# A state-space scan and the block behind it: earlier first units, a reordered mixing block, and step sizes added on TensorE in the last sequence

## The chip, the cores and the metric

The kernel runs on one core of a Trainium2 chip, in one launch. The metric is device time in microseconds (us). Five engines work side by side, each through its own list in order: TensorE (PE in the profile, PEld for its weight loads), VectorE (DVE), ScalarE (ACT), GpSimd (POOL) and SyncE (SP, which here issues all DMAs). They meet only at semaphores.

## The reference, cut to what matters

`x` is (2, 1024, 256). The kernel computes `x1 = x + attn(moe(x))` and then `x1 + ffn(sample(x1))`. `attn` is two state-space scans (Mamba), one over the sequence and one over its reverse, whose outputs are mixed by a gate:

```
delta = softplus(dt @ dt_w + dt_b)                       # the step sizes
h_t = exp(delta_t * A) * h_(t-1) + (delta_t * u_t) * B_t # 16 states for each of 512 channels
y_t = sum over the states of h_t * C_t;  y = (y + uc * Dp) * silu(z);  y_f or y_b = y @ outproj
g = sigmoid([y_f, y_b] @ gate_w + gate_b);  attn = (g * y_f + (1 - g) * y_b) @ proj_w + proj_b
```

`sample` divides |x1| by its sum over the sequence, takes exp, divides again, sums up along the sequence, counts how many sums lie below a random value, and keeps the elements of x1 that are at least as large as the one at that place. `ffn` needs its result in two layouts (`xt_s`, `xm_s`), each cut in a high and a low float32r part.

## The kernel before, in words

Four phases follow each other: experts (until 229 us), scan (`mamba_phase`, 229 to 1090 us), mixing (`mix_phase`, 1090 to 1163 us), feed-forward (`ffn_phase`, to the end).

**Scan.** There are 4 sequences `k` (2 batches times 2 directions), each 1024 long, and 4 channel blocks `dc` of 128: 16 periods `w`. A period has 16 units `s`, each a 128x1024 tile (32 channels times 4 states); rows `r` of a period are its units. For a unit:
- ScalarE: the decay, exp(delta * A), into one of two PSUM slots `hs` (`decay`, L1055). It waits until the unit two before has left its slot.
- GpSimd: `dbu` = (delta * u) * B, from the replicated step sizes `rep` (`inputs`, L1125). It may be at most four units ahead of the scan.
- VectorE: the scan itself (L1199).
- The product with C, into `hc`: VectorE makes it (`weigh`, L1211), except in units 0, 4, 8, 12, which GpSimd weighs (L1131) after the dbu of three units later (`POOL_LAG`). ScalarE may reuse the `hs` slot of a GpSimd unit as soon as the scan is done, of the others after the product.
- TensorE: four units at a time are summed over the states (`add_states`, L952), after all four products, in the order half, unit, so that its four 32-column tiles follow each other.

Between the units ScalarE and GpSimd prepare the step size of the next period: TensorE's `t`, then Abs and Relu (L1021, L1022), Exp and Ln, then `step_add` (L710, the two parts of softplus added) and `step_du` (L716, times u) on GpSimd behind the dbu of units 6 and 7 (8 and 9 in each sequence's last period). SP stores the result and loads it back 32-fold (`dd_rows`, `rep`). TensorE does its other work at fixed places of the period (`pe_chores`): `skip` (L938) and `z` (L910) first, then, by group of units, projections of the neighbouring sequences: `o` (L920) in period 12, the first gates `g` (L931) in period 14. All results but `ysum` go through two PSUM banks in turn (`pb`); the next user of a bank waits until ScalarE has read the last one. ScalarE reads `z` at unit 4, `o` at units 7, 8, 10 and 11 of period 12, `g` at units 8 and 13 of period 14, with table loads round them. VectorE closes a period with `gate_out` (L1190) after the scan of unit 1 of the next.

For period 0 nothing is loaded back: TensorE replicates delta and delta*u (L903), 16 results, and ScalarE copies each to `rep` (L1036) ahead of the first four decays.

**Mixing.** `first` halves of the mix for batch 0 are already made in the scan. TensorE's list: project batch 0 (L1378), the output projection of sequence 3 (L1389, second half first), the gates of batch 1 (L1399, L1402), its projections (L1378), then 16 turns (L1418, four 128x128 transposes each): x1 and sampled x1 of batch 0, then of batch 1. VectorE's list: residuals of batch 0 (L1559), the whole sampling chain of batch 0 (L1578 to L1591), the mix (L1548, L1551), the same for batch 1, then the low parts of the last turns (L1625). ScalarE copies every turn out of PSUM; for the sampled x1 of batch 0 it copies twice, and GpSimd makes the low part from the second copy (L1529). GpSimd also makes yf - yb (L1518). x1's turns go through two tiles, whose stores (L1356) must land before they are filled again.

## Time and profile before

| what | value |
|---|---|
| median of 3 runs | 1525.18 us (1520.16 to 1525.98) |
| the profiled execution, its own time | 1525.6 us |
| its span, first to last instruction | 1523.8 us |
| busy share of the span | PE 79%, DVE 76%, POOL 60%, ACT 51% |
| mean granted TensorE clock | 0.878 of full speed |
| mean DMA rate | 110 GB/s |

Read it by stage: in the span's 40 slices of 38 us, DVE stands at 9 tenths from the eighth slice to the 28th, the scan, with POOL beside it; PE stands at 9 tenths in the first five and the last nine. The shares of the whole span therefore say little. All times below are us from the span's start. In a timeline the columns are start, duration, engine, line, operation, output<-inputs, count, and in brackets the idle time before it and who ended it.

### The profile page before, as it was taken

What the parts mean: (1) busy time and instruction counts of PE and PEld (TensorE: products, weight loads), DVE (VectorE), ACT (ScalarE), POOL (GpSimd) and SP (SyncE); (2) the same over time, 40 slices, a digit from 0 to 9 for tenths busy, and PEclk for the clock granted to TensorE, in tenths of its full rate; (3) what the DMA queues carried; (4) which work ended last, traced back from release to release, by engine and by line L of the source; (5) the groups of instructions that cost most, each with busy time, mean ns of one, the idle gap of its engine ahead of it and who ended that gap; (6) DMA issues with size and microseconds to landing.
All of it is one profiled execution on the core that took longest, in us unless ns stands there. A gap on an engine that the chain in (4) does not pass through costs nothing. (4 is left out here: it accounts for less than half of the span.)

```text
span 1523.8 us, 14635 instructions
## 1 busy us (share of the span) xinstructions
PE 1196.4 (79%) x4932; PEld 667.1 (44%) x4932; DVE 1150.8 (76%) x1020; ACT 776.8 (51%) x1036; POOL 908.4 (60%) x405
## 2 busy tenths in 40 slices
PE   5999977798739897549987375464577999999998
PEld 4788832233203232113332021121235778787887
DVE  4433355999999999999999999999676554544544
ACT  4434366567545676556675465464245533333440
POOL 4420016999999999999999999999533000000000
...
GB/s 195 42 124 111 28 48 172 152 110 104 107 262 125 117 145 148 104 193 193 91 104 100 234 117 217 114 117 49 57 14 180 0 139 0 139 0 102 22 38 72
DMA packets 41824, 167.20 MB, mean 110 GB/s; under 512 B 5521, under 2 KB 10129, under 8 KB 29346
## 3 DMA queue, kind: packets, MB, share of 16 engines
...
HBM read 134.43 MB, written 31.98 MB: 109 GB/s over the span
## 5 line engine op out<-in xcount | busy, mean ns | idle before, releaser
L1125 POOL TENSOR_TENSOR scan_dbu<-scan_rep,scan_bc 128x1024 f32<-128x1024 f32 x256 | 597.0, 2362 | 38.5 <-ACT scan_rep L1036 33.6
L1199 DVE TENSOR_TENSOR_SCAN scan_hs<-scan_hs,scan_dbu 128x1024 f32<-128x1024 f32 x192 | 439.1, 2287 | 17.3 <-ACT scan_hs L1055 17.1
L1055 ACT ACTIVATE scan_hs<-scan_rep,scan_neg_a 128x1024 f32<-128x1024 f32 x256 | 285.3, 1118 | 324.8 <-DVE scan_hc L1211 299.1
L952 PE MATMUL scan_ysum<-scan_hc,scan_sel 128*32 128x512 f32 x1024 | 176.8, 823 | 225.6 <-DVE scan_hc L1211 225.5
L1211 DVE TENSOR_TENSOR scan_hc<-scan_hs,scan_bc 128x1024 f32<-128x1024 f32 x192 | 234.9, 1223 | 6.1
L952 PEld LDWEIGHTS scan_ysum<-scan_hc,scan_sel 128*32 128x32 f32 x1024 | 36.6, 132 | 345.3 <-issue 345.3
L1131 POOL TENSOR_TENSOR scan_hc<-scan_hc,scan_bc 128x1024 f32<-128x1024 f32 x64 | 150.9, 2358 | 12.8 <-DVE scan_hc L1199 12.5
L1199 DVE TENSOR_TENSOR_SCAN scan_hc<-scan_hs,scan_dbu 128x1024 f32<-128x1024 f32 x64 | 145.8, 2278 | 9.0 <-ACT scan_hs L1055 8.7
L861 PE MATMUL scan_pb<-late_xin,scan_inwf 128*128 128x512 f32 x256 | 113.8, 598 | 0.0
L32 PE MATMUL ffn_sl<-ffn_tanh_s,xm_s 128*128 128x512 f32 x384 | 106.0, 411 | 2.3 <-DVE ffn_tanh_s L1926 2.3
L32 PE MATMUL moe_first<-moe_x_s,moe_w_s 128*128 128x512 f32 x384 | 97.7, 397 | 8.3 <-DVE moe_w_s L412 8.3
L418 DVE TENSOR_TENSOR moe_first<-scan_bc,moe_first 128x512 f32<-128x512 f32 x48 | 33.3, 695 | 92.5 <-ACT scan_bc L330 55.6
L1746 PE MATMUL ffn_oy<-ffn_y,ffn_et 128*128 128x256 f32 x448 | 101.3, 379 | 0.8 <-DVE ffn_y L1946 0.8
L32 PE MATMUL ffn_lg<-phi_s,xt_s 128*128 128x512 f32 x384 | 97.9, 404 | 2.5 <-PEq L1279 1.8
L1909 DVE TENSOR_REDUCE ffn_lmax<-ffn_lsb 128x2 f32<-128x1024 f32 x32 | 39.0, 1220 | 78.1 <-ACT ffn_lsb L1840 78.1
L1746 PEld LDWEIGHTS ffn_oy<-ffn_y,ffn_et 128*128 128x128 f32 x448 | 84.9, 190 | 13.5 <-DVE ffn_y L1946 1.3
L32 PEld LDWEIGHTS moe_first<-moe_x_s,moe_w_s 128*128 128x128 f32 x384 | 73.7, 193 | 25.1 <-issue 9.2
L32 PE MATMUL moe_second<-moe_hid_s,moe_w_s 128*128 128x512 f32 x288 | 75.4, 398 | 5.8 <-DVE moe_hid_s L423 5.6
L32 PEld LDWEIGHTS ffn_lg<-phi_s,xt_s 128*128 128x128 f32 x384 | 71.2, 191 | 18.4 <-issue 3.4
L861 PEld LDWEIGHTS scan_pb<-late_xin,scan_inwf 128*128 128x128 f32 x256 | 47.5, 190 | 67.5 <-issue 67.5
L32 PEld LDWEIGHTS ffn_sl<-ffn_tanh_s,xm_s 128*128 128x128 f32 x384 | 69.4, 188 | 15.7 <-DVE ffn_tanh_s L1926 3.0
L330 ACT ACTIVATE scan_bc<-moe_first 128x512 f32<-128x512 f32 x48 | 28.8, 599 | 89.2 <-PE moe_first L32 89.2
...
## 6 DMA issues: line engine op xcount, KB each, us to landing
...
```

What stands on the lines that cost most here:

```text
L32: mm = nc.tensor.matmul(out, lhs[x], rhs[y], start=first and i == 0, stop=last and i == 2)
L330: nc.scalar.activation(act_h[:, g % 2, :], first[:, g % 3, 0, :], ACT.Silu if g % UNITS < SU else ACT.Gelu).then_inc(act_done, 1)
L418: nc.vector.tensor_tensor(first[:, g % 3, 1, :], act_h[:, g % 2, :], first[:, g % 3, 1, :], ALU.mult).then_inc(hid_done, 1)
L861: mm = nc.tensor.matmul(out, inwf[:, q % IWR, c, t, :], xin[k % 2][:, c, h * CT + t:h * CT + t + CT], start=(t == 0 and c == 0), stop=(t = ...
L952: mm = nc.tensor.matmul(ysum[i * D32:(i + 1) * D32, h, :], sel[:], hc[:, (s0 + i) % HCR, h * CT:(h + 1) * CT], start=False, stop=last, til ...
L1055: nc.scalar.activation(hs[:, s % HSR, :], rep[:, e % REPS, 0, :], ACT.Exp, scale=neg_a[:, k % 2, NI * dc + i, r // NI:r // NI + 1]).then_i ...
L1125: nc.gpsimd.tensor_tensor(dbu[:, s % DBR, :], rep[:, e % REPS, 1, :], bc[:, j, 0, :], ALU.mult).then_inc(dbu_done, 1)
L1131: nc.gpsimd.tensor_tensor(hc[:, s % HCR, :], hc[:, s % HCR, :], bc[:, s % UPP // NI, 1, :], ALU.mult).then_inc(pool_hc_done, 1)
L1199: nc.vector.tensor_tensor_scan(states, hs[:, s % HSR, :], dbu[:, s % DBR, :], 0.0, ALU.mult, ALU.add).then_inc(scan_done, 1)
L1211: nc.vector.tensor_tensor(hc[:, s % HCR, :], hs[:, s % HSR, :], bc[:, r // NI, 1, :], ALU.mult).then_inc(hc_done, 1)
L1746: mm = nc.tensor.matmul(bank[:, b * DM:(b + 1) * DM], et[:, b, j, m * P:(m + 1) * P], y[:, j, b, :], start=(j == 0), stop=(j == JT - 1))
L1909: nc.vector.tensor_reduce(lmax[:, m, :], lsb[:, m % 2], AX_X, ALU.max, negate=True).then_inc(small, 1)
```

## The change

Three things, none of which changes what is computed (sums of float32 are formed in another order).

**First units.** In period 0 ScalarE makes the first four decays straight from the replicated delta in PSUM, two Exp of 512 columns each, instead of copying it; only delta*u is copied. VectorE makes the dbu of units 0 and 1 itself. For units 4 and on of that period delta comes back through DRAM: SP stores it and loads it (without delta*u) before the later rows of B and C.

**Last sequence.** In periods 12, 13, 14 TensorE adds the two parts of the next step size (two float32 products with the identity for each half, key `a`), after the sum of units 0 to 3; ScalarE copies the result to `dd` at unit 6; GpSimd's `step_du` comes after the dbu of unit 9, and it has no `step_add` there. GpSimd weighs units 0, 3, 7, 10, 13. In period 15 TensorE makes three of four parts of sequence 3's output projection for the second half before the last group (`op`, in the two `pb` banks, which stay reserved over the phase), and the last group is added unit by unit.

**Mixing.** The output projection only adds the missing part for the second half. yf - yb moves to VectorE, between the steps of batch 0's sampling, and the mix and the sampling are interleaved. The normalising pass (L1579) is left out: the running sum is of the unnormalised values and the reciprocal is multiplied in the comparison, against the random value less 0.001. The turns of sampled x1 of batch 0 come first, then those of its low part `xt_s[1]` (TensorE turns it, ScalarE copies it: 20 turns instead of 16, each copied once), then x1 of both batches, then sampled x1 of batch 1. x1's turns have four tiles. The first piece of `phi` is loaded and cut first, and the Exp table is loaded right after the last Sigmoid.

```diff
+POOL_UNITS, LATE_POOL_UNITS = (0, 3, 7, 10, 13), (0, 4, 8, 12)
...
+def late_step(w):
+    return w < DC * (GROUPS - 1) or w % DC == DC - 1
...
+    return r in (LATE_POOL_UNITS if late_step(s // UPP) else POOL_UNITS)
...
+    total = [("a", k, p + 1, h) for h in range(HALVES)] if r == 1 and not late_step(DC * k + p) else []
...
+    partial = [("op", k, cc, 0) for cc in range(KC)] if not more and (p, r) == (DC - 1, NJ - 1) else []
+    return partial + total + (old.get((p, r), []) if done else []) + (new.get((p, r), []) if more else []) + step + gates
...
+TOTAL_AT = 6
+POOL_STEP_AT, LATE_POOL_STEP_AT, TOTAL_POOL_STEP_AT = (6, 7), (8, 9), (None, 9)
...
+        self.banks = ctx.enter_context(nc.psum_tensor("late_banks", [P, 2, CT], F32))
...
+        pb = late.banks
...
+        def wait_delta(eng, w):
+            if w == 0 or late_step(w - 1):
+                eng.wait_ge(delta_done, own_adds(w))
+            else:
+                freed(eng, *(("a", *divmod(w, DC), h) for h in range(HALVES)))
...
+                kinds = slice(0, 1 if w == 0 else 2)
+                wait_delta(sp, w)
+                if w > 0:
+                    sp.wait_ge(du_done, w + 1)
+                sp.dma_start(dd_rows[w % 2][:, kinds], dd[:, kinds]).then_inc(dd_out, 16)
...
+                kinds = 1 if w == 0 else 2
+                sp.wait_ge(dd_out, 16 * (w + 1))
...
+                src = dd_rows[w % 2][i * D32:(i + 1) * D32, 0:kinds].rearrange("d k t -> d (k t)")
+                sp.dma_start(rep[:, e % REPS, 0:kinds].rearrange("p k t -> p (k t)"),
+                             src.unsqueeze(1).to_broadcast([D32, NG, kinds * SEQ])).then_inc(rep_in[e % REPS], 16)
...
-            for j in range(1, NJ):
+            store_step(0)
+            load_rows(0, 1)
+            for i in range(NI):
+                load_rep(0, i)
+            for j in range(2, NJ):
                 load_rows(0, j)
...
+            def step_total(k, dc, h):
+                out, done = claim(("a", k, dc, h))
+                pe.wait_ge(soft, (HALVES + 2) * (DC * k + dc + 1))
+                freed(pe, *(("t", k, dc, i) for i in range(HALVES)))
+                for i in range(2):
+                    mm = nc.tensor.matmul(out, ident[:], dd[:, i, h * CT:(h + 1) * CT], start=(i == 0), stop=(i == 1))
+                mm.then_inc(done, 1)
...
+            def out_partial(k, cc, _):
+                out, _ = claim(("op", k, cc, 0))
+                pe.wait_ge(yg_done, DC * (k + 1) - 1)
+                pe.wait_ge(outw_in, 16 * (k + 1))
+                for dc in range(DC - 1):
+                    nc.tensor.matmul(out, outw[:, dc, cc * P:(cc + 1) * P], uc[:, k % 2, dc, CT:2 * CT], start=(dc == 0), stop=False)
...
-                        pe.wait_ge(hc_done, by_dve(s + 1))
+                if s0 + NI < UNITS_ALL:
+                    for i in range(NI):
+                        wait_product(s0 + i)
                 last = s0 % UPP == UPP - NI
+                if s0 + NI == UNITS_ALL:
+                    for i in range(NI):
+                        s = s0 + i
+                        wait_product(s)
+                        for h in range(HALVES):
+                            mm = nc.tensor.matmul(ysum[i * D32:(i + 1) * D32, h, :], sel[:],
+                                                  hc[:, s % HCR, h * CT:(h + 1) * CT],
+                                                  start=False, stop=last, tile_position=(0, i * D32))
+                        mm.then_inc(ysum_done, 1)
+                    return
...
-                wait(act, dd_out, 16 * (w - 1))
+                wait(act, dd_out, 16 * w)
...
-                for kind in (1, 0):
-                    for h in range(HALVES):
-                        x, free = ready(act, "r", i, kind, h)
-                        nc.scalar.activation(rep[:, i, kind, h * CT:(h + 1) * CT], x, ACT.Copy).then_inc(free, 1)
+                for h in range(HALVES):
+                    x, free = ready(act, "r", i, 1, h)
+                    nc.scalar.activation(rep[:, i, 1, h * CT:(h + 1) * CT], x, ACT.Copy).then_inc(free, 1)
+            def step_total(k, dc, h):
+                x, free = ready(act, "a", k, dc, h)
+                nc.scalar.activation(dd[:, 0, h * CT:(h + 1) * CT], x, ACT.Copy).then_inc(free, 1)
...
-                    wait_rep(act, e)
+                if NI <= s < 2 * NI or w > 0 and r < NI:
+                    act.wait_ge(rep_in[e % REPS], 16 * (e // REPS + 1))
...
-                nc.scalar.activation(hs[:, s % HSR, :], rep[:, e % REPS, 0, :], ACT.Exp,
-                                     scale=neg_a[:, k % 2, NI * dc + i, r // NI:r // NI + 1]).then_inc(da_done, 1)
+                scale = neg_a[:, k % 2, NI * dc + i, r // NI:r // NI + 1]
+                if s < NI:
+                    for h in range(HALVES):
+                        x, free = ready(act, "r", i, 0, h)
+                        nc.scalar.activation(hs[:, s % HSR, h * CT:(h + 1) * CT], x, ACT.Exp, scale=scale).then_inc(free, 1)
+                else:
+                    nc.scalar.activation(hs[:, s % HSR, :], rep[:, e % REPS, 0, :], ACT.Exp, scale=scale).then_inc(da_done, 1)
...
+                    if r == TOTAL_AT and not late_step(w):
+                        for h in range(HALVES):
+                            step_total(k, p + 1, h)
...
-                    inputs(s)
+                    if s >= DVE_INPUTS:
+                        inputs(s)
...
+            def inputs(s):
+                wait_du(dve, s)
+                dve.wait_ge(bc_in[0], 2 * 16)
+                nc.vector.tensor_tensor(dbu[:, s % DBR, :], rep[:, s, 1, :], bc[:, 0, 0, :], ALU.mult).then_inc(dbu_done, 1)
...
+                    if UPP * w + r < DVE_INPUTS:
+                        inputs(r)
                     scan(UPP * w + r)
...
-        dif = uc[:, 1, 0:KC, :]
-        whole = uc[:, 1, KC:2 * KC, :].rearrange("p k (h t) -> p (k h) t", h=CB)
-        turn_sb = first.inwz
-        pg = ps("pg", [P, CB, KC, CT])
+        dif = late.y_first
+        turn_sb = [tile[:, q, :] for tile in (first.inwz, first.dtw_wide) for q in range(2)]
+        pg = ps("pg", [P, KC, CT])
...
+        TURNS = [(kind, b, j) for kind, b in (("high", 0), ("low", 0), ("x1", 0), ("x1", 1), ("high", 1)) for j in range(TG)]
+        X1_TURNS = [g for g, key in enumerate(TURNS) if key[0] == "x1"]
...
+            sp.dma_start(kept["phi"][:], a["phi"][:, :, 0:CT]).then_inc(kept["loaded_phi"], 16)
             sp.dma_start(iota[:], a["iota"].partition_broadcast(P)).then_inc(consts_in, 16)
             sp.dma_start(x1_late[:], a["xT"][:, :, SEQ:2 * SEQ]).then_inc(loaded_x, 16)
             sp.dma_start(kept["ident"][:], a["ident"]).then_inc(consts_in, 16)
-            sp.dma_start(kept["phi"][:], a["phi"][:, :, 0:CT]).then_inc(kept["loaded_phi"], 16)
...
+                    g = X1_TURNS[TG * b + j]
+                    sp.wait_ge(turn_read[g % 2], g // 2 + 1)
+                    sp.dma_start(x1_rows[:, b, 2 * j:2 * j + 2, :], turn_sb[j].rearrange("p (m d) -> p m d", m=2)
...
+                    for dc in range(DC - 1 if h else 0, DC):
+                        mm = nc.tensor.matmul(late_bank(cc) if h else pp[:, cc, :], outw[:, dc, cc * P:(cc + 1) * P],
+                                              uc[:, 1, dc, h * CT:(h + 1) * CT], start=(dc == 0), stop=(dc == DC - 1))
...
-            def turn(g):
-                b, kind, j = g // (2 * TG), g // TG % 2, g % TG
-                if kind == 0:
+            def turn(kind, b, j):
+                g = TURNS.index((kind, b, j))
+                if kind == "x1":
                     pe.wait_ge(res_done, KC * CB * (b + 1))
+                elif kind == "high":
+                    pe.wait_ge(xm_done, KC * (b + 1))
                 else:
-                    pe.wait_ge(xm_done, KC * (b + 1))
+                    pe.wait_ge(xt_low, KC * (b + 1))
                 if g >= 2:
                     pe.wait_ge(turn_read[g % 2], g // 2)
                 for q in range(4):
                     cc, m = q % 2, 2 * j + q // 2
-                    src = x1[b][:, cc, :] if kind == 0 else xm_t[b][:, cc, :]
-                    mm = nc.tensor.transpose(tr[:, g % 2, q * P:(q + 1) * P], src[:, m * P:(m + 1) * P], kept["ident"][:])
+                    rows = slice(m * P, (m + 1) * P)
+                    src = {"x1": x1[b][:, cc, rows], "high": xm_t[b][:, cc, rows], "low": xt_s[1][:, cc, b, rows].bitcast(F32)}[kind]
+                    mm = nc.tensor.transpose(tr[:, g % 2, q * P:(q + 1) * P], src, kept["ident"][:])
                 mm.then_inc(turned, 1)
...
-                    if b or j >= 2:
-                        act.wait_ge(x1_stored[j % 2], 16 * (b * TG // 2 + j // 2))
-                    nc.scalar.activation(turn_sb[:, j % 2, :], tr[:, g % 2, :], ACT.Copy).then_inc(turn_read[g % 2], 1)
+                if kind == "x1":
+                    if b:
+                        act.wait_ge(x1_stored[j % 2], 16 * TG // 2)
+                    nc.scalar.activation(turn_sb[j], tr[:, g % 2, :], ACT.Copy).then_inc(turn_read[g % 2], 1)
...
+                    copied = nc.scalar.activation(xm_s[kind == "low"][:, b, 2 * j:2 * j + 2, :],
+                                                  tr[:, g % 2, :].rearrange("p (m d) -> p m d", m=2), ACT.Copy)
+                    copied.then_inc(turn_high if b else turn_read[g % 2], 1)
...
+            act.wait_ge(kept["loaded_phi"], 16)
+            nc.scalar.activation(kept["phi_s"][0][:], kept["phi"][:], ACT.Copy).then_inc(phi_high, 1)
...
             sigmoids(0)
+            sigmoids(1)
+            nc.scalar.preload_act_table_set("exp_and_others")
             for u in range(KC):
                 piece_high(u)
-            sigmoids(1)
...
+            for key in TURNS[:-TG]:
+                turned_out(*key)
...
+            for key in TURNS[-TG:]:
+                if key[2] == 2:
...
-            pool.wait_ge(late.yf_in, 16)
-            pool.wait_ge(out_read, KC * CB)
-            for h in range(CB):
-                for k in range(KC):
-                    nc.gpsimd.tensor_tensor(own(k, h), forward(k, h), reverse(k, h), ALU.subtract).then_inc(dif_done, 1)
...
-            for j in range(TG):
-                g = TG + j
-                pool.wait_ge(turn_read[g % 2], g // 2 + 1)
-                tile = (slice(None), 0, slice(2 * j, 2 * j + 2), slice(None))
-                nc.gpsimd.tensor_tensor(xm_s[1][tile], whole[:, j, :].rearrange("p (m d) -> p m d", m=2),
-                                        xm_s[0][tile].bitcast(F32), ALU.subtract).then_inc(low_done, 1)
             piece_low(nc.gpsimd, pool, KC)
...
+            def difference(h):
+                dve.wait_ge(late.yf_in, 16)
+                dve.wait_ge(out_read, KC * (h + 1))
+                for k in range(KC):
+                    nc.vector.tensor_tensor(own(k, h), forward(k, h), reverse(k, h), ALU.subtract).then_inc(dif_done, 1)
...
+            def sums(b):
                 for cc in range(KC):
                     dve.wait_ge(exp2_done, KC * b + cc + 1)
-                each(lambda cc, s: nc.vector.reciprocal(s[:, 4:5], s[:, 3:4]))
...
-                each(lambda cc, s: nc.vector.tensor_tensor_scan(cum[:, cc, :], ones[:], share[:, cc, :], 0.0,
...
-                                                           ALU.mult, ALU.add))
+                each(b, lambda cc, s: nc.vector.reciprocal(s[:, 1:2], s[:, 3:4]))
+                each(b, lambda cc, s: nc.vector.tensor_tensor_scan(cum[:, cc, :], ones[:], share[:, cc, :], 0.0,
+                                                                   ALU.mult, ALU.add))
...
+                each(b, lambda cc, s: nc.vector.scalar_tensor_tensor(share[:, cc, :], cum[:, cc, :], s[:, 1:2],
+                                                                     rv[:, cc, b:b + 1].to_broadcast([P, SEQ]), ALU.mult, ALU.is_le,
+                                                                     accum_out=s[:, 4:5]))
...
+            link(nc.vector.tensor_scalar(rv[:], rv[:], 0.001, None, ALU.subtract))
...
+            sums(0)
+            difference(0)
             threshold(0)
+            difference(1)
+            mix(0)
+            choose(0)
+            mix(1)
             half_sum(0)
-            mix(0)
-            mix(1)
...
+            sums(1)
             threshold(1)
+            choose(1)
             half_sum(1)
```

## Rows read from the trace of the kernel before

**Rows 1.** Busy time of each engine while sequence 3 is scanned

```profile
core 0: us, PE busy (x) PEld busy (x) DVE busy (x) ACT busy (x) POOL busy (x), PEclk, DMA share, GB/s
877.00:1088.00 211.00, 114.41 (x392) 35.49 (x392) 204.01 (x116) 105.65 (x109) 206.24 (x91) 0.73 0.29 111
```

**Rows 2.** Timeline of DVE, start of period 12; the ends of periods 11 and 14

```profile
876.74 2.28 DVE L1199 TENSOR_TENSOR_SCAN scan_hc<-scan_hs,scan_dbu 128x1024 f32<-128x1024 f32 x1
878.93 2.27 DVE L1199 TENSOR_TENSOR_SCAN scan_hs<-scan_hs,scan_dbu 128x1024 f32<-128x1024 f32 x1
881.12 1.21 DVE L1190 TENSOR_TENSOR late_uc<-scan_ysum,scan_sz 128x1024 f32<-128x1024 f32 x1
...
886.83 2.29 DVE L1199 TENSOR_TENSOR_SCAN scan_hs<-scan_hs,scan_dbu 128x1024 f32<-128x1024 f32 x1
...
890.29 2.28 DVE L1199 TENSOR_TENSOR_SCAN scan_hc<-scan_hs,scan_dbu 128x1024 f32<-128x1024 f32 x1
...
1037.60 1.21 DVE L1190 TENSOR_TENSOR late_uc<-scan_ysum,scan_sz 128x1024 f32<-128x1024 f32 x1
```

**Rows 3.** Timeline of POOL, period 12: `step_add` after the dbu of unit 6

```profile
888.53 2.35 POOL L710 TENSOR_TENSOR scan_dd<-scan_dd 128x1024 f32<-128x1024 f32 x1
890.85 2.36 POOL L1125 TENSOR_TENSOR scan_dbu<-scan_rep,scan_bc 128x1024 f32<-128x1024 f32 x1
```

**Rows 4.** Timelines of PE, DVE, POOL and ACT at the start of the scan

```profile
241.39 3.80 PE L903 MATMUL scan_pb<-scan_dd,scan_hc 128*128 128x512 f32 x8 [0.60 <-ACT scan_rep L1036]
...
240.85 2.29 DVE L1199 TENSOR_TENSOR_SCAN scan_hc<-scan_hs,scan_dbu 128x1024 f32<-128x1024 f32 x1 [8.73 <-ACT scan_hs L1055]
...
262.53 2.30 DVE L1199 TENSOR_TENSOR_SCAN scan_hs<-scan_hs,scan_dbu 128x1024 f32<-128x1024 f32 x1 [2.41 <-ACT scan_hs L1055]
...
250.75 2.35 POOL L1125 TENSOR_TENSOR scan_dbu<-scan_rep,scan_bc 128x1024 f32<-128x1024 f32 x1 [2.03 <-ACT scan_rep L1036]
...
252.87 1.12 ACT L1055 ACTIVATE scan_hs<-scan_rep,scan_neg_a 128x1024 f32<-128x1024 f32 x1
```

**Rows 5.** Timeline of PE, periods 13 and 14: group sums and first gates

```profile
942.25 1.92 PE L952 MATMUL scan_ysum<-scan_hc,scan_sel 128*32 128x512 f32 x16 [0.75 <-DVE scan_hc L1211]
...
1010.22 7.13 PE L931 MATMUL scan_pb<-late_uc,scan_inwf 128*128 128x512 f32 x16
1020.24 3.49 PE L952 MATMUL scan_ysum<-scan_hc,scan_sel 128*32 128x512 f32 x16 [2.88 <-DVE scan_hc L1211]
```

**Rows 6.** Timeline of PE, the last group of the scan

```profile
1085.18 3.44 PE L952 MATMUL scan_ysum<-scan_hc,scan_sel 128*32 128x512 f32 x16 [8.93 <-DVE scan_hc L1211]
```

**Rows 7.** Mixing: timelines of PE and ACT, then three groups of DVE passes

```profile
1097.41 7.03 PE L1389 MATMUL mix_pg<-late_uc,late_outw 128*128 128x512 f32 x16
...
1129.90 3.70 PE L1378 MATMUL mix_tr<-late_uc,scan_inwf 128*128 128x512 f32 x8 [1.43 <-DVE late_uc L1551]
...
1135.59 1.28 ACT L1462 ACT_TABLE_LOAD   x1
...
1142.94 1.22 ACT L1472 ACTIVATE scan_inwz<-mix_tr 128x512 f32<-128x512 f32 x2 [2.71 <-DMA x_rows<-scan_inwz]
...
1156.90 1.97 PE L1418 MATMUL mix_tr<-ident,late_uc 128*128 128x128 f32 x8 [5.33 <-DVE late_uc L1591]
...
1163.22 2.04 PE L32 MATMUL ffn_lg<-phi_s,xt_s 128*128 128x512 f32 x4 [1.76 <-PEq L1279]
...
L1585 DVE SCALAR_TENSOR_TENSOR scan_bc<-mix_iota,mix_stat,scan_bc 128x1024 f32<-128x1024 f32 x4 | 6.9, 1752 | 0.1
L1582 DVE SCALAR_TENSOR_TENSOR scan_bc<-scan_bc,late_rv 128x1024 f32<-128x1024 f32 x4 | 5.8, 1487 | 0.1
L1579 DVE TENSOR_SCALAR scan_bc<-scan_bc,mix_stat 128x1024 f32<-128x1024 f32 x4 | 2.8, 750 | 0.1
```

**Rows 8.** Busy time while TensorE has nothing but turns

```profile
1144.00:1147.00 3.00, 2.59 (x12) 1.95 (x11) 2.97 (x4) 2.22 (x5) 1.03 (x1) 0.50 0.48 178
1149.00:1152.00 3.00, 2.42 (x15) 1.50 (x13) 2.96 (x5) 1.42 (x3) 3.00 (x2) 0.88 0.35 127
```

122 lines of the change are left out of this document (51 added, 71 removed).

## The prediction

> **What bounds the kernel now.** The slices of the page come first: PE full in the first and the last stage, DVE and POOL full in the scan between. So the next view is the busy time of the stage that the change touches most, sequence 3's scan [rows 1]: in 211 us DVE is busy for 204 and POOL for 206, both nearly full, ACT half, and TensorE's granted clock averages 0.73, a mixture of its two levels, 2.4 GHz (1.00) and 1.2 GHz (0.50). The timeline of DVE [rows 2] shows what a unit costs. A unit whose product GpSimd makes takes 2.19 us (876.74 to 878.93), one whose product DVE makes 3.46 (886.83 to 890.29), `gate_out` 1.1. Periods 12 to 14 take 156.5 us from `gate_out` to `gate_out` (881.12 to 1037.60), 52.2 each. On POOL a step has a pitch of 2.32 us (888.53 to 890.85) [rows 3]; 16 dbu, 4 products, `step_add` and `step_du` make 22 steps, 51.0 us: POOL is 1.2 us from being the bound. The start of the scan and the mixing block are chains over several engines, where the waits in brackets tell what came last [rows 4, 7]. The feed-forward phase starts at 1163.22 and is not touched; what is gained ahead of it moves it as a whole.
>
> **First units.** Now TensorE makes four replicated results in 3.80 us, 0.95 each, then stands 0.60 because ScalarE, in the decay (1.12), does not free a bank [rows 4]: 4.4 us per unit. After, ScalarE's decay is two half Exp on the results themselves (0.6 to 0.7 each, as its copies), so the chain is TensorE's 3.8 us per unit. The first scan gains the 1.1 us of the decay, the fourth decay, now 252.87 to 253.99, ends after three shorter rounds near 251.1. Behind it stand Abs and Relu of period 1, decay 4, and z, which TensorE starts later than ScalarE's table load ends: they move up by 1.8 us only, since z's own products need 1.7 us for each half. So unit 5's scan, which now waits 2.41 us for ScalarE until 262.53, comes at 260.8. POOL, without a gap from 250.75 on, now starts that unit 3 dbu when its replica is copied, near 249.25: 1.5 us earlier, and it feeds units 10 to 13 with little to spare. DVE's own two dbu (1.22 each, as its product) lie in its idle time. SP's store and four loads of delta start at 230.9, land some 6 us each behind one another, and are needed near 253: at nothing, with some 7 us of cover; the rows of B and C behind them are needed from 254 on. **Term: -1.5 us** (-0.5 to -2.5).
>
> **Last sequence.** Saved on DVE: one product in each of three periods, 3.46 - 2.19 = 1.27, in all -3.8. POOL's steps stay 22: the add leaves, the product comes, so its 51.0 us per period is a floor, but it starts each period several units ahead and can give that up for a while: the dbu of unit 6 is done at 888.5 [rows 3], 8 us before its scan. The price is a new chain. Times now from the scan of unit 0:
> - Unit 3 is GpSimd's. Its scan ends at 12.4 (10.1 to 12.4), its product by GpSimd at 15.0. Before, DVE's own product let TensorE's first sum begin at 13.8 (942.25 in period 13, whose unit 0 is one period after 876.74), after 0.75 us of idling, at the high clock, 1.92 us; after 2.88 us of idling such a sum took 3.49, the low clock [rows 5]. z ends 0.75 us before 13.8, so TensorE now idles 2 to 3 us. I take the low clock in periods 12 and 14 and half of it in 13: the sum ends at 18.6 (17.7).
> - `a`: four float32 products of 512 columns. Eight such took 7.13 us right after a slow sum [rows 5], 0.89 each: 3.55 us, the second half ready at 22.3, copied (0.6) at 22.9, then decay 7 (1.12) at 24.0. Unit 7's scan is due at 23.0 (two units of 2.19, five of 3.46, `gate_out`). Stall 1.0 us in 12 and 14, 0.2 in 13. With all at the high clock none, with `a` also at the low one 3.5 more in each.
> - Behind the waiting ScalarE stand `o` and `g`, which need the banks that `a` holds. Period 12: `o` takes four products from 22.1, ready at 25.8, copied, decay 8 at 27.5, due at 26.2: 1.3. Period 14: two gates, ready at 29.3, a Sigmoid 0.7, table load 1.28, decay 9 at 32.4, due at 29.7; such a stall is 0.5 now: 2.2 more.
> - `step_du` moves from behind dbu 7 to behind dbu 9, with store and loads behind it on SP. The last period of each sequence has it there already; the next period's first dbu is 15 us later. At nothing.
>
> Sum 1.0 + 1.3 + 0.2 + 1.0 + 2.2 - 3.8 = 1.9. **Term: +2.0** (-1.7 with every step at the high clock, +12 with `a` at the low one).
>
> **End of the scan.** Now the last sum begins after 8.93 us of idling, at the low clock: 3.44 us on the path [rows 6]. After, `op` (six products, 5.3 us) runs from about 1076, in DVE's shadow, and keeps TensorE busy; then units 12 to 14 are added as they come. Unit by unit four passes of one column tile follow each other (16 in 1.92 us is four at a time, 0.43 to 0.48 a pass), so unit 15 still takes 1.8 us at the high clock. **Term: -1.4** (+2 if `op` is slow and the sums queue behind it).
>
> **Mixing** [rows 7]. TensorE's list, up to the end of the last projection (1133.6), has one gap, 1.43 us. Six of the eight products of 7.03 us leave: -5.2. VectorE's mix is now done before its projection is due, so the gap goes: -1.4; sum -6.6. VectorE's moved differences (4 x 0.65) lie where it waited for gates. From there the chain is ScalarE and VectorE: the table load of 1.28 is made earlier; the two passes of L1579 in batch 1 (1.4) are gone; and the eight passes of L1582 and L1585, 12.9 us, would take 10.0 at the 1.22 to 1.28 of such a pass without GpSimd's L1529 beside it, which is gone too: -2.9. The sampled x1 of batch 1 is ready 6.6 + 1.3 + 1.4 + 2.9 = 12.2 earlier, at 1144.7 instead of 1156.9. But ScalarE is free only from 1131.3 (1135.59, the load, two Exp of 1.2, less 6.6 and 1.3) and must by then have copied 16 turns. A turn of four transposes takes TensorE 0.97 us at the low clock (8 in 1.97) and 0.6 to 0.7 at the high one with the bank's return; with five slow and nine fast ones behind the two that wait ready, the chain ends at 1143.5, and x1's second batch must wait for a store (ScalarE now waits up to 2.71 us for one): 1145. Then a copy of 1.05 and the tail, as now 5 us from the first high turn to the feed-forward. So it starts near 1151.7. **Term: -11.3** (-8 to -13). Twenty turns instead of 16 lie in this chain.
>
> One rule speaks against it. While TensorE had only turns, its clock was 0.50 for 3 us at 86% busy, and then 0.88 [rows 8]: here they do raise it, late. The Trainium skill's TensorE: Matmul & The Clock Gate, Part 4 (PE-mode transpose), says that transposes do not count as busy work for the clock. By it all turns would stay slow and the total be 1.3 us more, 1514.7; the second row disagrees.
>
> **Sum.** 1525.6 (the profiled execution's own time; the median of the runs is 1525.18, 0.4 lower) - 1.5 + 2.0 - 1.4 - 11.3 = 1513.4.
>
> **Rivals.**
> - *Clean*: TensorE stays fast, `a` is in time. Last sequence -1.7: 1509.7. For: sums after 0.75 us of idling are fast. Against: 2.88 us was enough to slow one.
> - *Slow a*: it runs at the low clock in part, +7 instead of +2: 1518.4; the product of unit 3 is then the step to blame.
> - *Turns*: ScalarE's 20 copies and the stores become the mixing block's bound, its gain is 7: 1517.7. Against: the longest such wait is 2.71 us, with two tiles instead of four.
> - *Cold* (the other side): all added work of sequence 3 at 1.2 GHz. It decides if TensorE, busy half of the time there, never gets back to 1.00. `a` +12; `op` takes 10.3 us, until 1086.6, and four sums of 2.6 to 3.4 follow, 1098 instead of 1088.6: +9. Total 1525.6 - 1.5 + 12 + 9 - 11.3 = 1533.8. Against: eight products right after a slow sum ran fast [rows 5].
> - *Nothing at the front*: POOL's queue or SP's loads hold back period 0, 1514.9: inside the forecast's range.
>
> **How the numbers follow.** Forecast 0.58 (its own range 1509 to 1518), clean 0.15, slow 0.14, turns 0.08, cold 0.05. The range 1507.5 to 1521.5 holds all but cold and the edges. 0.5% of 1525.18 is 7.6 us, about what a measurement of this kernel can tell from no change: faster means below 1517.6. That is nearly all of the forecast and of clean, under half of slow and of turns: 0.76; slower is cold, 0.04; the rest 0.20.
>
> **What would show it.** Feed-forward starts near 1151; between the second projection and it no GpSimd pass L1529; xm of batch 1 ready 2 us or less before ScalarE reaches it. In periods 12 to 14 DVE waits for the decay of units 7, 8 and 9, with `a`'s copies just before; without such waits the periods take 51 us and the stall term was wrong. The first scan comes near 239.7, unit 5's near 260.8; if that one has not moved, z or the loads bound it. A last sum of 3.4 us after the last product says that `op` did not keep the clock up. I am wrong if the mixing block gives less than 8 us or sequence 3 costs over 8.

## The result, and the profile after

The kernel after takes 1511.18 us (median of 5 runs, 1510.42 to 1512.48), the kernel before 1525.18 beside it (1520.07 to 1526.24): a ratio of 0.9918, 95% interval 0.9897 to 0.9939. The profiled execution takes 1510.97 us with a span of 1509.2, against 1525.6 and 1523.8. The prediction was 1513.4 in 1507.5 to 1521.5.

The two spans, cut at the same instructions. `du` is `step_du` of period 0 on VectorE, the last step before the scan's first units.

| stage | before | after | difference | predicted |
|---|---|---|---|---|
| start to `du` | 230.90 | 233.23 | +2.3 | 0 |
| `du` to `gate_out` of period 11 | 650.22 | 647.39 | -2.8 | -1.5 |
| periods 12 to 14 | 156.48 | 155.00 | -1.5 | +2.0 |
| period 15 | 51.17 | 49.43 | -1.7 | -1.4 |
| `gate_out` of period 15 to the mixing block | 1.70 | 1.69 | 0 | 0 |
| mixing block to the feed-forward's first product | 72.75 | 61.61 | -11.1 | -11.3 |
| feed-forward | 360.58 | 360.85 | +0.3 | 0 |

Start of the scan in the kernel after, timelines of PE, then DVE (the counterparts of rows 4; columns: start, length, engine, line, operation, tiles, shape, count, idle before it with its releaser):

```profile
234.60 16.37 PE L941 MATMUL late_banks<-scan_dd,scan_hc 128*128 128x512 f32 x32 [5.97 <-DVE scan_dd L740]
...
238.81 1.22 DVE L1278 TENSOR_TENSOR scan_dbu<-scan_rep,scan_bc 128x1024 f32<-128x1024 f32 x1 [4.35 <-ACT scan_rep L1102]
240.69 2.29 DVE L1286 TENSOR_TENSOR_SCAN scan_hc<-scan_hs,scan_dbu 128x1024 f32<-128x1024 f32 x1 [0.65 <-ACT scan_hs L1129]
...
261.45 2.30 DVE L1286 TENSOR_TENSOR_SCAN scan_hs<-scan_hs,scan_dbu 128x1024 f32<-128x1024 f32 x1 [2.14 <-ACT scan_hs L1131]
```

TensorE makes all 32 matmuls of the replicas without a gap. Unit 5's scan comes 28.2 us after `du` (31.6 before) and still waits for ScalarE, whose decay stands behind the reading of z.

Period 12 and the wait of period 14 in the kernel after, timelines of PE, ACT, DVE (rows 2, 3 and 5):

```profile
891.43 1.92 PE L1019 MATMUL scan_ysum<-scan_hc,scan_sel 128*32 128x512 f32 x16 [2.43 <-POOL scan_hc L1211]
893.28 3.70 PE L949 MATMUL late_banks<-scan_dd,scan_ident 128*128 128x512 f32 x8
...
897.02 0.60 ACT L1106 ACTIVATE scan_dd<-late_banks 128x512 f32<-128x512 f32 x1 [1.12 <-PE late_banks L949]
897.52 1.11 ACT L1131 ACTIVATE scan_hs<-scan_rep,scan_neg_a 128x1024 f32<-128x1024 f32 x1
...
899.37 2.28 DVE L1286 TENSOR_TENSOR_SCAN scan_hc<-scan_hs,scan_dbu 128x1024 f32<-128x1024 f32 x1
902.16 2.30 DVE L1286 TENSOR_TENSOR_SCAN scan_hs<-scan_hs,scan_dbu 128x1024 f32<-128x1024 f32 x1 [0.51 <-ACT scan_hs L1131]
...
931.86 1.21 DVE L1271 TENSOR_TENSOR late_uc<-scan_ysum,scan_sz 128x1024 f32<-128x1024 f32 x1
...
1008.91 2.30 DVE L1286 TENSOR_TENSOR_SCAN scan_hs<-scan_hs,scan_dbu 128x1024 f32<-128x1024 f32 x1 [1.79 <-ACT scan_hs L1131]
```

The first sum begins after 2.43 us of idling and still takes 1.92 us; it idles 2.18 us before that of period 13 and 2.28 before that of 14, and both take 1.92. `a` follows at once, is copied by 897.6, and the decay of unit 7 ends 0.7 us before its scan (899.37) begins: no wait.

End of the scan in the kernel after, PE and DVE (rows 6):

```profile
1074.10 5.42 PE L985 MATMUL late_banks<-late_uc,late_outw 128*128 128x512 f32 x12
1079.45 2.09 PE L1012 MATMUL scan_ysum<-scan_hc,scan_sel 128*32 128x512 f32 x12
1083.11 1.90 PE L1012 MATMUL scan_ysum<-scan_hc,scan_sel 128*32 128x512 f32 x4 [1.56 <-DVE scan_hc L1298]
...
1085.05 1.22 DVE L1271 TENSOR_TENSOR late_uc<-scan_ysum,scan_sz 128x1024 f32<-128x1024 f32 x1 [2.00 <-PE scan_ysum L1012]
```

Mixing in the kernel after, PE, ACT, DVE, then two groups of DVE passes (rows 7). No pass of GpSimd lies beside VectorE's threshold passes any more, and the L1677 and L1680 groups take 1.28 us a pass where rows 7 have 1.49 and 1.75:

```profile
1119.44 3.60 PE L1477 MATMUL mix_tr<-late_uc,scan_inwf 128*128 128x512 f32 x8
...
1139.05 1.21 ACT L1572 ACTIVATE scan_inwz<-mix_tr 128x512 f32<-128x512 f32 x2 [2.93 <-DMA x_rows<-scan_dtw]
...
1140.00 0.27 DVE L1695 TENSOR_SCALAR half_sum<-mix_stat 128x1 f32<-128x1 f32 x2
...
1148.35 2.04 PE L32 MATMUL ffn_lg<-phi_s,xt_s 128*128 128x512 f32 x4 [1.74 <-PEq L1368]
...
L1680 DVE SCALAR_TENSOR_TENSOR scan_bc<-mix_iota,mix_stat,scan_bc 128x1024 f32<-128x1024 f32 x4 | 5.0, 1282 | 0.1
L1677 DVE SCALAR_TENSOR_TENSOR scan_bc<-scan_bc,mix_stat,late_rv 128x1024 f32<-128x1024 f32 x4 | 5.0, 1280 | 0.0
```

The `half_sum` row marks the time at which the sampled x1 of batch 1 (xm) is ready: 53.3 us after the block's start at 1086.74. Below, stages are read in each run's own trace as in the table; most repeat to 0.1 us from run to run, while whole times scatter by some us.

### The profile page after: what moved, and what is told of

Its sections match the earlier page's. It is cut to its first block and busy times, and to the rows that moved or that the text cites. A ratio compares the mean times of both kernels' runs of the same rounds, so it can differ in the third digit from the quotient of the medians.

```text
span 1509.2 us, 14727 instructions
## 1 busy us (share of the span) xinstructions
PE 1202.4 (80%) x4972; PEld 670.6 (44%) x4972; DVE 1144.5 (76%) x1020; ACT 776.6 (51%) x1038; POOL 888.9 (59%) x395
## 5 line engine op out<-in xcount | busy, mean ns | idle before, releaser
L1286 DVE TENSOR_TENSOR_SCAN scan_hs<-scan_hs,scan_dbu 128x1024 f32<-128x1024 f32 x189 | 432.2, 2287 | 15.7 <-ACT scan_hs L1131 14.1
L1131 ACT ACTIVATE scan_hs<-scan_rep,scan_neg_a 128x1024 f32<-128x1024 f32 x252 | 280.8, 1118 | 303.2 <-DVE scan_hc L1298 276.4
L1019 PE MATMUL scan_ysum<-scan_hc,scan_sel 128*32 128x512 f32 x1008 | 169.6, 804 | 208.5 <-DVE scan_hc L1298 193.1
L1298 DVE TENSOR_TENSOR scan_hc<-scan_hs,scan_bc 128x1024 f32<-128x1024 f32 x189 | 231.1, 1223 | 6.0
L1211 POOL TENSOR_TENSOR scan_hc<-scan_hc,scan_bc 128x1024 f32<-128x1024 f32 x67 | 157.7, 2353 | 10.2 <-DVE scan_hc L1286 9.8
L1286 DVE TENSOR_TENSOR_SCAN scan_hc<-scan_hs,scan_dbu 128x1024 f32<-128x1024 f32 x67 | 152.7, 2279 | 2.0 <-POOL scan_dbu L1205 1.0
L899 PE MATMUL late_banks<-late_xin,scan_inwf 128*128 128x512 f32 x256 | 114.5, 601 | 0.0
L899 PEld LDWEIGHTS late_banks<-late_xin,scan_inwf 128*128 128x128 f32 x256 | 47.8, 191 | 68.9 <-issue 68.9
L1945 ACT ACTIVATE ffn_lsb<-ffn_lg 128x512 f32<-128x512 f32 x64 | 37.9, 594 | 71.8 <-PE ffn_lg L32 71.6
```

The costliest lines, as they stand in the source:

```text
L899: mm = nc.tensor.matmul(out, inwf[:, q % IWR, c, t, :], xin[k % 2][:, c, h * CT + t:h * CT + t + CT], start=(t == 0 and c == 0), stop=(t = ...
L1019: mm = nc.tensor.matmul(ysum[i * D32:(i + 1) * D32, h, :], sel[:], hc[:, (s0 + i) % HCR, h * CT:(h + 1) * CT], start=False, stop=last, til ...
L1131: nc.scalar.activation(hs[:, s % HSR, :], rep[:, e % REPS, 0, :], ACT.Exp, scale=scale).then_inc(da_done, 1)
L1211: nc.gpsimd.tensor_tensor(hc[:, s % HCR, :], hc[:, s % HCR, :], bc[:, s % UPP // NI, 1, :], ALU.mult).then_inc(pool_hc_done, 1)
L1286: nc.vector.tensor_tensor_scan(states, hs[:, s % HSR, :], dbu[:, s % DBR, :], 0.0, ALU.mult, ALU.add).then_inc(scan_done, 1)
L1298: nc.vector.tensor_tensor(hc[:, s % HCR, :], hs[:, s % HSR, :], bc[:, r // NI, 1, :], ALU.mult).then_inc(hc_done, 1)
```

## The experiments

**1. The new mixing block alone**, on the scan of before. `op` is gone with the scan, so the block makes all eight products again.

```diff
-for dc in range(DC - 1 if h else 0, DC):
+for dc in range(DC):
```

> The kernel before with the new mixing block alone (its second projection still makes all eight products, the scan is that of before). Theory (the mixing block gains by its own chain, whatever lies ahead): block start to feed-forward start goes from 72.8 us to 61.6 + 5.2 for the six products that op had taken = 66.8 us, a gain of 6.0; total near 1519.5. Rival (the ScalarE and VectorE chain sets the end, TensorE's list has room): 61.6 us here too, a gain of 11, total near 1514.5.

Measured 1519.52 us, ratio 0.9955 (0.9941 to 0.9969). The block takes 66.4 us, xm is ready at 58.4. The theory holds: TensorE's list sets the time up to the last projection.

**2. The first units added to it.** Sequence 3 and the end of the scan stay as before.

> The same mixing block and the new first units; sequence 3 and the end of the scan as before. Theory: from the du of period 0 to gate_out of period 11 is 3.4 us shorter than before at unit 5 and 2.8 at the end, so 2.8 us below the run with the mixing alone, near 1516.7. Rival (what the trace of after shows is lost again between periods 0 and 11, since POOL has only 1.2 us of slack in a period): 1.5 us or less below it. If the 2.3 us by which the first scan's inputs came later in the profiled run of after belong to the change, the front up to du is longer by 2.3 here too; theory says that they do not and that it is like before within 1 us.

Measured 1517.54 us, ratio 0.9932 (0.9918 to 0.9946). From `du` to `gate_out` of period 11 it takes 646.9 us; run 1, with the old start, takes 647.2, the profiled run of before 650.2. So the 2.8 us that theory expected between these two runs do not show (0.3), as its rival said, while the medians differ by 2.0; one pair of executions does not settle it. PE at the first replicas, in before (rows 4 begin behind it), run 1, run 2:

```profile
232.27 8.52 PE L903 MATMUL scan_pb<-scan_dd,scan_hc 128*128 128x512 f32 x12 [5.97 <-DVE scan_dd L716]
```

```profile
234.61 6.99 PE L905 MATMUL late_banks<-scan_dd,scan_hc 128*128 128x512 f32 x12 [5.97 <-DVE scan_dd L718]
```

```profile
234.50 17.80 PE L941 MATMUL late_banks<-scan_dd,scan_hc 128*128 128x512 f32 x32 [5.97 <-DVE scan_dd L740]
```

After the same 5.97 us of idling the same matmuls start at the low clock and rise at another point in each execution: 32 take 16.37 us in after and 17.80 here. Runs with a late rise are compared with each other, and runs with an early one: unit 5's scan comes 31.6 after `du` in before and 29.6 here (late), 30.1 in run 1 and 28.2 in after (early). The new start gives 2.0 and 1.9 us there, and 1.7 and 1.6 at unit 15 of period 0 (63.9 and 62.2; 62.4 and 60.8).

How much of it is left at `gate_out` 11 is not shown. The three executions with the old start (before, runs 1 and 9) need 650.2, 647.2 and 649.6 us from `du` to there (mean 649.0), ten with the new one 645.1 to 647.4 (mean 647.0), run 10 left out. The means differ by 2.0, but run 1 is level with after (647.4): after loses its lead in periods 1 and 3, 54.1 and 52.7 us against 52.0 and 51.7, where VectorE waits longer for the decay of unit 5. The scan of that unit in period 1, after and run 1:

```profile
314.79 2.30 DVE L1286 TENSOR_TENSOR_SCAN scan_hs<-scan_hs,scan_dbu 128x1024 f32<-128x1024 f32 x1 [1.34 <-ACT scan_hs L1131]
```

```profile
316.64 2.30 DVE L1201 TENSOR_TENSOR_SCAN scan_hs<-scan_hs,scan_dbu 128x1024 f32<-128x1024 f32 x1 [0.36 <-ACT scan_hs L1057]
```

Before, with the old start, waits 1.28 us there, and run 2, with the new one, 0.36: the long wait comes with either start.

The front up to `du` is 230.7 to 230.9 or 233.0 to 233.4 us, whatever the kernel: before, run 4 and run 11 have the first, run 1 with the old start the second. So the +2.3 of the table is not the change's.

**3. Sequence 3 as before.**

```diff
 def late_step(w):
-    return w < DC * (GROUPS - 1) or w % DC == DC - 1
+    return True
```

> The kernel after with sequence 3 as before (GpSimd adds the two parts, four C products in every period). Theory (the change of sequence 3 gains 1.5 us in periods 12 to 14, as its stalls are 0.2 to 0.6 us each except one of 1.8): 1.5 us slower than after, periods 12 to 14 take 156.5 us, total near 1512.7. Rival (my recorded term, +2.0): 2 us faster than after, near 1509.

Measured 1510.90 us, ratio 0.9893 (0.9878 to 0.9909). Periods 12 to 14 take 156.48 us, as before the change, 1.5 more than after. The whole time does not show so small a term (1510.90 us here, 1511.18 after); the stage does. My recorded +2.0 is wrong.

**4. Without op**, the last sums still unit by unit.

```diff
-    partial = [("op", k, cc, 0) for cc in range(KC)] if ... else []
+    partial = []
-for dc in range(DC - 1 if h else 0, DC):
+for dc in range(DC):
```

> The kernel after without op: the six products of the last output projection are made in the mixing block again, the last sums still come unit by unit. Theory (they are on TensorE's list ahead of the last projection, nothing hides them, and without them TensorE is idle before the last sums): mixing +5.2 us, the last sums at 1.2 GHz, unit 15's 1.9 us instead of 1.9 since it is slow in both or fast in neither; wait before the last gate_out 2.0 to 3.7 us; total +5.2 to +6.9, near 1517. Rival (the block is bound by ScalarE and VectorE): +1 or less.

Measured 1515.99 us, ratio 0.9938 (0.9924 to 0.9951). The block takes 68.1 us (after 61.6), but period 15 still takes 49.43. PE:

```profile
1072.59 2.80 PE L1012 MATMUL scan_ysum<-scan_hc,scan_sel 128*32 128x512 f32 x8 [1.12 <-POOL scan_hc L1211]
1076.95 1.90 PE L1012 MATMUL scan_ysum<-scan_hc,scan_sel 128*32 128x512 f32 x4 [1.56 <-DVE scan_hc L1298]
1080.41 1.90 PE L1012 MATMUL scan_ysum<-scan_hc,scan_sel 128*32 128x512 f32 x4 [1.56 <-DVE scan_hc L1298]
```

The passes of units 12 to 14, with pauses of 1.1 to 1.6 us between them, are enough by themselves: the granted clock is 1.00 from 1072 us on. `op` is worth its products in the block and nothing at the end of the scan. Period 15 takes 49.4 us in all nine executions that sum unit by unit. The low clock that I expected for these sums did not come.

**5. a without the fifth product.**

```diff
-    return r in (LATE_POOL_UNITS if late_step(s // UPP) else POOL_UNITS)
+    return r in LATE_POOL_UNITS
```

> The kernel after with four C products in every period; TensorE still adds the two parts of the step sizes in periods 12 to 14. Theory (the gain of sequence 3 is the fifth product, 1.27 us on VectorE in each period; the add on TensorE only makes room for it): periods 12 to 14 take 156.5 us or up to 1 more for stalls behind a, 1.5 to 2.5 more than after. Rival (GpSimd's 22 steps of 2.32 us are already what bounds these periods at 51.7, so taking one away is the gain): 155 or less without the fifth product.

Measured 1512.62 us, ratio 0.9923 (0.9899 to 0.9947); periods 12 to 14 take 156.49 us. The theory holds: taking the add from GpSimd gives nothing by itself; it now waits for VectorE eleven times in the three periods, up to 1.1 us, 9.0 in all (after: twice, 1.0 in all).

**6. The fifth product without a.** `late_step` is always true, and `pool_unit` keeps the five units by the old condition.

> The kernel after with five C products on GpSimd in periods 12 to 14 and GpSimd still adding the two parts of the step sizes: 23 steps of 2.32 us, 53.4 us a period. Theory (GpSimd starts period 12 some 8 us ahead and loses 3 us of it in each period, so the room made by the add is not needed in three periods): 155 to 157 us for periods 12 to 14, period 15 as in after. Rival (GpSimd becomes the bound at once): 160 us, 53.4 each.

Measured 1514.38 us, ratio 0.9926 (0.9904 to 0.9949); periods 12 to 14 take 161.1 us. The rival, nearly: 4.6 us more than before. DVE and PE in period 12:

```profile
910.75 2.29 DVE L1291 TENSOR_TENSOR_SCAN scan_hc<-scan_hs,scan_dbu 128x1024 f32<-128x1024 f32 x1 [2.85 <-PE scan_ysum L1024]
```

```profile
907.02 3.64 PE L1024 MATMUL scan_ysum<-scan_hc,scan_sel 128*32 128x512 f32 x16 [3.80 <-POOL scan_hc L1216]
```

GpSimd's lead is in dbu, not in products: the product of unit 7 comes a step late, TensorE waits 3.80 us for it, sums at the low clock, and VectorE waits for the slot. Over the three periods GpSimd stands only once, for 0.6 us, so it is the bound. The two halves of this part only pay together: -1.5 with both, 0 and +4.6 with one. Whether a later place for the add, behind unit 7's product, would have cost less was not tried.

**7. a twice**, each product issued twice (the result is the same).

```diff
-for i in range(2):
+for i in (0, 1, 0, 1):
```

> The kernel after with each of a's products issued twice, eight where there were four (7.1 us, which is also what four take at 1.2 GHz); the sum is computed twice and comes out the same. In after the decay of unit 7 ends 0.7 us before its scan is due. Theory (that is all the slack, ScalarE's list holds the decays behind a): VectorE waits 2.9 us for the decay of unit 7 and 0.7 more for that of unit 8, 3 to 3.6 in each of periods 12 to 14, in all +10 us: about 165 us for the three. Rival (ScalarE catches up in the idle time that it has): +4 or less.

Measured 1523.26 us, ratio 0.9993 (0.9978 to 1.0007); periods 12 to 14 take 166.2 us, +11.2. DVE:

```profile
900.00 2.29 DVE L1286 TENSOR_TENSOR_SCAN scan_hc<-scan_hs,scan_dbu 128x1024 f32<-128x1024 f32 x1 [2.67 <-ACT scan_hs L1131]
903.50 2.30 DVE L1286 TENSOR_TENSOR_SCAN scan_hs<-scan_hs,scan_dbu 128x1024 f32<-128x1024 f32 x1 [1.21 <-ACT scan_hs L1131]
```

The theory holds: the chain over sum, `a`, its copies and the decay is as tight as predicted. The three periods take 3.5, 3.0 and 4.8 us more than in after; in the last the sum itself also ran at the low clock (3.24 us after 3.98 of idling). Against before it is +9.7. The prediction's +12 for `a` at the low clock, which had the sums slow as well, was a fair price.

**8. op, but the last four units summed together.**

> The kernel after with op but with the last four units summed together, as before the change. Theory (the chip holds TensorE's clock up for the 3.6 us between op's end and the last product, as op's 5.4 us went before): the sum of 16 passes takes 1.9 us, as unit 15 alone does, and period 15 stays 49.4 us. Rival (op is too long ago, it is the passes of units 12 to 14 in between that keep the clock up): the sum takes 3.4 to 3.6 us and period 15 takes 51.1 us, +1.6.

Measured 1514.35 us, ratio 0.9928 (0.9903 to 0.9954); period 15 takes 50.43 us. Neither: PE

```profile
1083.06 2.75 PE L1008 MATMUL scan_ysum<-scan_hc,scan_sel 128*32 128x512 f32 x16 [3.69 <-DVE scan_hc L1287]
1087.61 2.90 PE L1466 MATMUL mix_pp<-late_uc,scan_inwf 128*128 128x512 f32 x3 [1.79 <-PEq L656]
```

After 3.69 us of idling the sum takes 2.75 us, between 1.92 and 3.64, and the mixing block's first projections are slow too (2.90 for three; 3.67 for eight in after), so that the block takes 64.4 us with xm ready at 54.9. `op` alone does not hold the clock in this execution; summing unit by unit saves 1.0 here and 1.6 up to xm in the block.

**9. GpSimd beside the threshold passes**, on the kernel of run 1. Six subtractions into a gate tile that nothing reads any more.

```diff
+pool.wait_ge(y_done, CB * KC)
+pool.wait_ge(exp2_done, 2 * KC)
+for i in range(6):
+    wait(pool, beside, i - 1)
+    nc.gpsimd.tensor_tensor(gate[:, 1, i % 2, :], gate[:, 0, 0, :], gate[:, 0, 1, :], ALU.subtract).then_inc(beside, 1)
```

> The kernel with the new mixing block alone, and beside VectorE's threshold passes of batch 1 six GpSimd subtractions of 512 columns (about 2.15 us each) into a gate tile that nothing reads any more. Theory (in the kernel before, L1529's passes on GpSimd slow the passes of VectorE that lie beside them, 1.22 to 2.2 us): from the start of the scan pair to the end of the sampling it takes 3 to 5 us longer than in the run with the mixing alone, single passes of 1024 columns show 2.1 to 2.3 us instead of 1.28, and xm of batch 1 is ready 62 to 63 us after the block's start instead of 58.4. Rival (the long passes of before have another cause, such as the DMA stores of x1 at that time): 58.4 us still, all passes 1.28. The scan is the old one: from du of period 0 to gate_out of period 11 it takes 647 to 650 us.

Measured 1523.99 us, ratio 0.9991 (0.9978 to 1.0003). xm is ready at 64.1 instead of 58.4, and the block takes 70.5 instead of 66.4. DVE:

```profile
1139.29 6.42 DVE L1590 TENSOR_TENSOR_SCAN scan_bc<-mix_ones,scan_bc 128x1024 f32<-128x1024 f32 x2
1145.75 2.11 DVE L1595 SCALAR_TENSOR_TENSOR scan_bc<-scan_bc,mix_stat,late_rv 128x1024 f32<-128x1024 f32 x1
...
1147.79 2.28 DVE L1595 SCALAR_TENSOR_TENSOR scan_bc<-scan_bc,mix_stat,late_rv 128x1024 f32<-128x1024 f32 x1
```

The passes take 2.1 to 2.3 us instead of 1.28, and the pair of scans 6.42 instead of 4.48. The theory holds, and the effect is larger than it said: from the scans to the end of the sampling it takes 18.3 us instead of 12.6, 5.7 more (expected 3 to 5).

**10. More periods with a, and x1's turns first.**

```diff
-    return w < DC * (GROUPS - 1) or w % DC == DC - 1
+    return w == 0 or w % DC == DC - 1
-(("high", 0), ("low", 0), ("x1", 0), ("x1", 1), ("high", 1))
+(("x1", 0), ("high", 0), ("low", 0), ("x1", 1), ("high", 1))
```

> The kernel after with two more edits. (1) The turns of x1 of batch 0 come first, ahead of high and low, so that its stores are done when the turns of x1 of batch 1 want the same tiles. Theory (the wait of 2.9 us for a store lies on ScalarE's way to the last turns, xm of batch 1 is ready 53.3 us after the block's start): the wait goes and the block takes 59.0 to 59.8 us instead of 61.6. Rival (the tail from xm to the feed-forward is what it is): 61 or more. (2) TensorE adds the step sizes and GpSimd takes five C products also in periods 1, 2, 4 to 6 and 8 to 10. Theory (they gain like periods 12 and 13 where TensorE is half idle, 0.5 to 1 us in periods 2, 6 and 10, and lose where it is busy for 46 of 51 us, as in periods 4 and 8): the periods of before changed by -0.5 to -1 in 2, 6 and 10 and by 0 to +2 in the others. Rival (all gain 0.5 to 1): 5 us in all.

Measured 1525.24 us, ratio 1.0007 (0.999 to 1.0023). The scan up to `gate_out` 11 takes 664.2 us, 17 more; periods 2, 6 and 10, which I expected to gain, take 54.0, 53.6 and 53.7 us instead of 51.8. DVE in period 1:

```profile
323.85 2.29 DVE L1286 TENSOR_TENSOR_SCAN scan_hc<-scan_hs,scan_dbu 128x1024 f32<-128x1024 f32 x1 [1.98 <-ACT scan_hs L1131]
332.23 2.30 DVE L1286 TENSOR_TENSOR_SCAN scan_hs<-scan_hs,scan_dbu 128x1024 f32<-128x1024 f32 x1 [2.65 <-ACT scan_hs L1131]
```

Where TensorE also makes the next sequence's `u`, `a` pushes those products and the copies behind them on ScalarE back, and the decays with them; that is my reading of the lists, and no run takes it apart. Both views of mine on this edit were wrong: none of the periods changed here gains, and 4 and 8, where I expected the loss, lose least of them (0.5 and 0.7 us). The part only pays in sequence 3. The other edit did what it should: no wait for a store, block 58.9 us.

Period 14, whose scan code is that of after, takes 55.73 us here instead of 52.98. PE, then DVE:

```profile
1010.35 3.64 PE L1019 MATMUL scan_ysum<-scan_hc,scan_sel 128*32 128x512 f32 x16 [3.99 <-POOL scan_hc L1211]
1013.92 4.71 PE L949 MATMUL late_banks<-scan_dd,scan_ident 128*128 128x512 f32 x8
...
1020.31 2.29 DVE L1286 TENSOR_TENSOR_SCAN scan_hc<-scan_hs,scan_dbu 128x1024 f32<-128x1024 f32 x1 [1.80 <-ACT scan_hs L1131]
...
1028.69 2.30 DVE L1286 TENSOR_TENSOR_SCAN scan_hs<-scan_hs,scan_dbu 128x1024 f32<-128x1024 f32 x1 [2.64 <-ACT scan_hs L1131]
```

This is what the prediction feared: z ran wholly at the high clock and was done earlier, so TensorE idled 3.99 us, the sum took 3.64, `a` was slow in part, and the decays of units 7 and 9 came late. It costs 2.75 us. Of the 21 first sums in periods 12 to 14 of the seven executions with both halves of the part, 19 took 1.92 or 1.93 us, and two were slow, this one and that of run 7, both in period 14.

**11 and 12. x1's turns first alone (the second edit of run 10); and with it the first gates taken at unit 10.** The diff is of run 12.

```diff
-FIRST_GATE_AT = {8: 0, 13: 1}
+FIRST_GATE_AT = {10: 0, 13: 1}
```

> The kernel after with the turns of x1 of batch 0 first, and nothing else. Theory (the scan is that of after, the block was 58.9 us with this order beside another scan): block 58.9 us against 60.3 to 63.1 in the five runs that had op and the fast first projections, total 1 to 4 us below after, near 1508.5. Rival (what made it 58.9 was a luckier clock of the turns): above 60.3.

> The same, and in period 14 ScalarE takes the first pair of gates after the decay of unit 10 instead of unit 8. In after, VectorE waits 1.79 us there for the decay of unit 9, which stands behind two Sigmoids and two table loads. Theory: both gates are ready by then, the wait goes, period 14 takes 51.2 to 51.7 us instead of 52.98, total 1.5 us lower still, near 1507. Rival (the banks come free later, so the second pair of gates delays the sum of group 2 and with it the slots of units 14 and 15, or the two Sigmoids now hold up unit 11 instead): 53 us or more.

Measured 1509.80 us, ratio 0.9897 (0.9877 to 0.9916), and 1506.67 us, ratio 0.9878 (0.9860 to 0.9896). The block takes 59.2 and 59.0 us; in five runs with `op` and the old order it took 60.3, 60.3, 60.4, 61.6 and 63.1 (run 8 with its slow first projections left out), with waits for a store of 1.5 to 3.8 us. Period 14 takes 51.74 us instead of 52.98. ACT and DVE of run 12, where the two gates are ready when ScalarE comes to them and the wait of 1.79 us is gone:

```profile
1009.66 0.69 ACT L1136 ACTIVATE scan_inwf<-late_banks,late_gb 128x512 f32<-128x512 f32 x1
1010.25 0.68 ACT L1136 ACTIVATE scan_xw<-late_banks,late_gb 128x512 f32<-128x512 f32 x1
...
1013.40 2.30 DVE L1286 TENSOR_TENSOR_SCAN scan_hs<-scan_hs,scan_dbu 128x1024 f32<-128x1024 f32 x1 [0.54 <-ACT scan_hs L1131]
```

Run 12 is below both kernels by the ratio against before (0.9878; after 0.9918). The two were not timed side by side and the intervals end 0.0001 apart (0.9896 and 0.9897), so the step from after rests on the stages: 1.2 us in period 14, 1.1 to 4.1 in the block.

## Why the prediction was right, and where it was not

The forecast was 2.2 us above the median measured, and in the range; the sum held because the largest term did. In the profiled run the stages of the scan differ from it by -1.3, -3.5 and -0.3, mixing and feed-forward by +0.2 and +0.3, 4.6 us in all, and a front that ran 2.3 us longer by chance took back half of that: the closeness of the total is in part luck.

- **First units, -1.5:** right in size as far as period 0: -1.9 and -2.0 at unit 5 between executions of the same clock (forecast 262.53 - 260.8 = 1.7), -1.6 and -1.7 at unit 15. At `gate_out` 11 the means differ by -2.0, but run 1 is level with after (run 2), so that the term lasts to there is not shown. What I had not seen is that the granted clock at this place differs from execution to execution by as much as the term; the -2.8 of the table is such a pair. SP's store and loads cost nothing: no decay of period 0 waits for them.
- **Last sequence, +2.0:** wrong, it is -1.5 (run 3). The step that failed: "TensorE now idles 2 to 3 us. I take the low clock in periods 12 and 14". The idling was 2.43, 2.18 and 2.28 us and every sum took 1.92 us. From the one slow sum after 2.88 us [rows 5] I had carried the low clock down to 2.2; the fast row was after 0.75 us. The trace of before held more sums between the two, which I did not show:

```profile
404.56 1.92 PE L952 MATMUL scan_ysum<-scan_hc,scan_sel 128*32 128x512 f32 x16 [1.97 <-DVE scan_hc L1211]
...
523.84 2.45 PE L952 MATMUL scan_ysum<-scan_hc,scan_sel 128*32 128x512 f32 x16 [2.73 <-DVE scan_hc L1211]
...
576.00 3.41 PE L952 MATMUL scan_ysum<-scan_hc,scan_sel 128*32 128x512 f32 x16 [2.73 <-DVE scan_hc L1211]
```

  They say that at 2 to 3 us it can be either, not that it is slow. With the high clock the working gave -1.7, the rival *Clean*, and its stalls came nearly as worked out: 0.51 us for unit 8 in period 12 (the working with the high clock gives 0.6), 1.79 for unit 9 in period 14 (2.0; the forecast itself had 1.3 and 2.7). The chain is real: 0.7 us of slack at unit 7, and runs 7 and 10 show the price when it is used up. `step_du` moved at no cost. GpSimd's 51.0 us a period are about what periods 12 and 13 take, 51.24 and 50.78; period 14 takes 52.98.
- **Product and add:** run 6 shows that the product needs the add's room at once. In the prediction GpSimd "starts each period several units ahead and can give that up for a while"; that was not so for products, but with 22 steps it did not matter.
- **End of the scan, -1.4:** -1.7, right in size. That `op` keeps TensorE busy is not the cause: without it the end is the same (run 4), and with it but with one sum 1.0 us is lost (run 8). It is the passes unit by unit.
- **Mixing, -11.3:** -11.1. TensorE's list: -6.6 forecast, the last projection ends 36.3 us after the block's start instead of 43.1, -6.8. Of it `op` gives 5.1 (xm at 53.3 against 58.4 in run 1). From there to xm: 1.3 + 1.4 + 2.9 = 5.6 forecast, 23.3 to 17.0 = 6.3 measured; the pass that the 2.9 rests on, slowed by GpSimd, is shown by run 9. The tail from xm to the feed-forward: 7.0 forecast, 8.4 here, 7.0 to 7.2 in three of the other runs; the wait for a store, forecast to end 54.5 us after the block's start (1145 on the clock of before), ended at 52.3, and is what runs 10 to 12 take away.
- **Rivals:** *Slow a* and *Cold* did not happen in the profiled execution: `a` took 3.70 us in each period. In period 14 of run 10 it took 4.71. *Clean* is what happened to the last sequence. *Turns* is true as far as the waits for stores go, and cost 1 to 4 us, not 4.3.
